# Third attention of an image tower: the order in which its token groups are combined, normalised and projected

## The reference

```python
    h = _layernorm(h + _L0_ffn_ref(h, ...), axis=-1)   # ends in the expert mixture
    h = _layernorm(h + _L1_attn_ref(h, ...), axis=-1)  # the third attention

    # _L1_attn_ref: 12 heads of 16 channels, 37 tokens an image
    qkv = jnp.einsum('bnc,oc->bno', x, w_qkv)...
    attn = jnp.einsum('bhid,bhjd->bhij', q, k) * scale[None, :, None, None]
    attn = jnp.where(diag[None, None, :, :], -jnp.inf, attn)
    attn = jax.nn.softmax(attn, axis=-1)
    out = jnp.einsum('bhij,bhjd->bhid', attn, v)
    out = out @ w_proj.T + b_proj
    return out + x
```

## Time and profile before

| | us |
|---|---|
| median of 3 runs | 1878.59 |
| the runs | 1878.59, 1874.66, 1887.67 |
| the profiled execution | 1880.07 |
| span of its instructions | 1878.3 |

### The profile page before, as it was taken

One profiled execution on the slowest core, in us unless ns is written; L12 is line 12 of the kernel. 1 busy time (PEld: TensorE's weight loads), 2 busy tenths in 40 slices (PEclk: granted clock), 3 DMA queues, 4 the chain that ended last, 5 costly groups with the idle time before them and its releaser, 6 DMA issues.

```text
span 1878.3 us, 33999 instructions
## 1 busy us (share of the span) xinstructions
PE 1609.9 (86%) x11941; PEld 1493.8 (80%) x11941; DVE 1067.8 (57%) x2975; ACT 812.7 (43%) x1979; POOL 512.2 (27%) x1259
## 2 busy tenths in 40 slices
PE   5898995984988998899977999788989999789980
PEld 5787874984877898889977999688878898779970
DVE  4665555332654777457765444367755778634437
ACT  2453531432555554345433555344543544245520
POOL 3255244004432121522232000453126123300031
PEclk8765855995557999999889999879989989899995
DMA  5020001551088000100004676300011000167731
GB/s 154 26 78 28 25 21 54 149 161 27 24 269 249 2 1 18 47 18 1 16 16 133 202 224 216 96 15 2 1 48 34 1 11 20 29 191 229 224 94 35
DMA packets 87756, 149.78 MB, mean 80 GB/s; under 512 B 7380, under 2 KB 58883, under 8 KB 87590
## 3 DMA queue, kind: packets, MB, share of 16 engines
q1 hardware_dynamic: 81254, 135.35, 23.6%
q0 software_dynamic: 6336, 12.26, 2.3%
HBM read 106.59 MB, written 41.05 MB: 79 GB/s over the span
## 4 chain that ended last, share of the span: by engine, by line
PE 54%; issue 22%; DVE 16%; ACT 4%; POOL 2%; DMA 2%; DVEq 0%; POOLq 0%; SPq 0%; ACTq 0%
PE ps_proj L1065 10%; PE ps_proj L1188 6%; PE ps_score L1259 5%; PE ps_proj L1079 5%; PE ps_proj L1242 4%; PE ps_o L1160 4%; PE ps_pt L1030 4%; PE ps_score L1116 4%; PE ps_o L1150 3%; PE ps_score L1127 2%; DVE prob L1593 2%; DVE prob L1590 2%; DVE negmax L1592 2%; PE ps_proj L1046 1%; PE ps_turn L1008 1%
## 5 line engine op out<-in xcount | busy, mean ns | idle before, releaser
L1259 PE MATMUL ps_score<-w,hid 128*112 128x192 f32 (+2 forms) x1680 | 300.2, 330 | 6.9 <-DVE x L1902 6.9
L1259 PEld LDWEIGHTS ps_score<-w,hid 128*112 128x112 f32 (+2 forms) x1680 | 272.8, 177 | 8.9 <-DVE x L1902 8.7
L1383 ACT ACTIVATE hid<-ps_proj 128x224 f32<-128x224 f32 (+2 forms) x360 | 137.8, 385 | 267.7 <-PE ps_proj L1242 267.7
L1490 POOL TENSOR_SCALAR tmp<-rs,var 111x1 f32<-111x1 f32 x110 | 40.5, 368 | 607.2 <-DVE rs L1561 606.8
L1448 POOL DMA_INDIRECT tin<-rows_out,idx x66 | 67.3, 1019 | 467.1 <-issue 363.8
L1030 PE MATMUL ps_pt<-const,prob 111*111 111x111 f32 x660 | 126.7, 310 | 36.7 <-ACT probt L1371 24.8
L1188 PE MATMUL ps_proj<-wo,ot 128*111 128x192 f32 (+1 forms) x616 | 141.5, 380 | 3.9 <-ACT ot L1349 3.7
L1030 PEld LDWEIGHTS ps_pt<-const,prob 111*111 111x111 f32 x660 | 94.8, 202 | 56.8 <-issue 23.7
L1371 ACT ACTIVATE probt<-ps_pt 111x333 f32<-111x333 f32 x176 | 78.8, 448 | 127.1 <-PE ps_pt L1030 126.6
L1160 PEld LDWEIGHTS ps_o<-v,probt 111*111 111x111 f32 x1056 | 126.1, 191 | 0.4
L1188 PEld LDWEIGHTS ps_proj<-wo,ot 128*111 128x111 f32 (+1 forms) x616 | 113.8, 206 | 15.5 <-issue 12.8
(11 more groups left out here) (256 smaller groups left out, 4212.2 us busy)
## 6 DMA issues: line engine op xcount, KB each, us to landing
w_in<-w_all_dram SPq DMA_DIRECT2D x130, 384.0 KB, 3.5
w<-w_all_dram SPq DMA_DIRECT2D x50, 576.0 KB, 5.2
rows_in<-zero SPq DMA_DIRECT2D x1, 12320.0 KB, 46.1
rows_out<-zero SPq DMA_DIRECT2D x1, 9240.0 KB, 79.9
tin<-rows_in SPq DMA_DIRECT2D x36, 224.0 KB
rows_out<-tout SPq DMA_DIRECT2D x36, 168.0 KB
patch<-patches_dram SPq DMA_DIRECT2D x11, 333.0 KB, 3.0
wo<-wo_all_dram SPq DMA_DIRECT2D x6, 576.0 KB, 3.9
```

The costliest lines, as they stand in the source:

```text
L1259: last = pe.matmul(bank[0:n, 0:C], hid[:, i % 2, m, at:at + n], w2[:, slot, m, :], start=(m == 0), stop=(m == FC - 1))
L1383: act.activation(hid[:, i % 2, m, 0:n], bank[:, 0:n], ACT.Relu if b.tile is None else ACT.Gelu).then_inc(taken, 1)
```

## The change

The blocks of the third attention become (0), (1,2), (3,4), (5,6,7), (8,9,10). Ahead of its first scores now stand: GAT 0, 1, 2, then COMB 0, COMB 1, NC 0, A 0, COMB 2, GAT 3, 4, 5, NC 1, the projections of block 0 and V 0, then A 1, NC 2, A 2. In round 0, QK of block 1 moves from the end of the round to right behind GAT 6, COMB 3, GAT 7. The table `DIAG_COMB` says which groups are combined in which round: one a round, but groups 6 and 7 both in round 3. NC c and A c come a round later, and A now always stands in `slots[1]`, ahead of PV. Nothing that is computed changes.

```diff
-DIAG_BLOCKS = [(0, 1), (1, 2), (3, 2), (5, 2), (7, 2), (9, 2)]
+DIAG_BLOCKS = [(0, 1), (1, 2), (3, 2), (5, 3), (8, 3)]
+DIAG_COMB = {0: [3], 1: [4], 2: [5], 3: [6, 7], 4: [8], 5: [9], 6: [10]}
...
         if a == DIAG:
+            for c in DIAG_COMB.get(n - 1, ()):
+                slots[0].append(("prev", ("NC", c)))
+                slots[1].append(("A", c))
             if n == 0:
-                slots[0] += combine(1) + combine(2) + [x for g in (1, 2) for x in (("prev", ("NC", g)), ("A", g))]
-            else:
-                slots[0] += [("prev", ("NC", n + 2))] * (n + 2 < G)
-            if n + 3 < G:
-                slots[0 if n else 2] += combine(n + 3)
-            if n and n + 2 < G:
-                slots[1 if last else 2].append(("A", n + 2))
+                slots[0].append(("prev", ("GAT", 6)))
+            for c in DIAG_COMB.get(n, ()):
+                slots[0] += combine(c)
         if n + 1 < G:
             slots[2].append(("V", n + 1, 0))
         if a == DIAG and last and b + 1 < len(s.blocks):
-            slots[2] += [("QK", b + 1, j) for j in (0, 2, 1, 3)]
+            slots[0 if n == 0 else 2] += [("QK", b + 1, j) for j in (0, 2, 1, 3)]
...
-    out = neigh_lead() if a == NEIGH else first_block(a) if last_stage[0] == "ffn" else []
+    out = neigh_lead() if a == NEIGH else []
+    if a == DIAG:
+        out += first_block(a) + [("A", 1), ("prev", ("NC", 2)), ("A", 2)]
...
-    out += [("GAT", 0), ("GAT", 1), ("COMB", 0), ("GAT", 2), ("GAT", 3), ("NC", 0), ("GAT", 4), ("next", ("A", 0))]
+    out += [("GAT", 0), ("GAT", 1), ("GAT", 2), ("COMB", 0), ("COMB", 1), ("NC", 0), ("next", ("A", 0)), ("COMB", 2),
+            ("GAT", 3), ("GAT", 4), ("GAT", 5), ("NC", 1)]
```

## The result

| us | before | after |
|---|---|---|
| median of 20 runs each, timed in turn | 1888.12 | 1877.63 |
| lowest to highest | 1873.97 to 1895.85 | 1863.73 to 1887.08 |
| the profiled execution | 1880.07 | 1864.46 |
| span of its instructions | 1878.3 | 1862.7 |

The ratio is 0.9949, with a 95% interval of 0.9930 to 0.9969. That is 9.6 us off 1888.12 (5.9 to 13.2), where 7.2 had been forecast; 1877.63 lies in the range of 1862 to 1880, within 1% as the 0.92 said. It lies near the upper end, though the gain was larger than forecast, because the kernel before now has a median of 1888.12 where the three runs that the forecast started from had 1878.59. The ratio is what tests the forecast: 1872 for 1878.59 is 0.9965. The profiled execution of the new kernel is nearly the fastest of its 20 runs.

The account below looks back on a forecast made before the run. Third attention: a chain through all engines before 464 us, then PE, mostly at 1.2 GHz. Terms -10.7 (head) + 6.0 (rounds 3, 4) + 1.3 (wide QK) - 3.8 (rest) = -7.2 us, forecast 1872, 8 in 10 within 1862 to 1880.

Parts of the forecast that it names:

- the 0.92: Whole kernel: the forecast chance that the measured time changes by less than 1%, 18.8 us, either way.
- The head: Third attention up to S 1: S 0 4.8 us later, S 1 10.7 us earlier, that lead kept at S 3.
- Rounds 3 and 4: PE waits on DVE at OT 2 and A 7, and on ACT for group 7's norm: +6.0 us together.
- the wide QK: End of round 4: QK of block 3, three groups wide, costs 20 x 0.06 = 1.3 us more.
- the list of signs: Expected in the new trace: S 0 near 444, S 1 near 453, waits at OT 2 (round 3) and A 7, 80 QK matmuls.
- Rounds 5 to 10: One QK block fewer -4.2 us, one turn wait fewer -1.4, a short round lost +1.8: net 3.8 us less.
- one such short round is lost: Rounds 5 to 10: the round behind a QK block is short from a higher clock; one block fewer costs 1.8 us.
- its bound of 5.6: Rounds 5 to 10: upper end of the forecast saving, bounded at 2 to 5.6 us less.
- The lead given back: Round 4: turns and POOL norms stall PE another 5 us, net gain 0 to 2, about 1878; chance 0.17.
- T5 starting at the low clock: Start of T5: clock stays at 0.5, costing some 11 us, net +4, 1883; chance 0.09.
- Stalls covered or the clock helps: Rounds 3 and 4 cost nothing, gain 13.2 us, or 15 with a full-clock stretch: about 1864; chance 0.2.

Follow-up runs that it names:

- the mended kernel: The changed kernel with COMB 6 and COMB 8 behind QK at the end of rounds 2 and 4, and A 7 behind PV 3; ratio 0.9904, rerun 0.9911.

## Why the prediction was right, and where a step was not

**The head: right.** The norm on POOL was forecast 1.3 us later. The first projection came 13.5 us behind the first gather, 12.1 before, so 1.4 later. S 0 was forecast 4.8 us later and came 5.0 later; S 1 10.7 earlier, and came 9.9 earlier (458.38 - 426.65 = 31.73, where it was 463.57 - 421.90 = 41.67). Round 1 was 1.0 us shorter (7.84 for 8.81), and the lead at S 3 was 10.9. The runs bear out the reason: the head alone has 10.6 at S 3, and QK's place is 1.0 of the gain at S 1. That the first profile agrees to 0.2 us is luck. The eleven profiles with the new head have S 3 between 52.4 and 58.4 us behind the first gather, with a median of 55.4; against the one profile of before that is a lead of 7.6 to 13.6, and of 10.6 at the median. What moves it is the late ACT in round 0 and the clock in rounds 1 and 2 (20.6 to 23.4 us), which the forecast took as fixed. In absolute time S 0 stood at 449.15 rather than "near 444" only because the first gather came 4.75 us later in that profile.

**Rounds 3 and 4, and the wide QK: right in the waits, and in sum partly by luck.** Foreseen were a wait at OT 2 of 1.8 us on DVE (1.62), a wait at A 7 of about 2 (2.02), something for ACT behind NC 7 before OT 2's bank is emptied (0.8; the wait at Y 2 is 1.30), and 1.3 for three groups' width. The three waits lie in round 4, that at OT 2 too, which the list of signs put in round 3. PE's idle time there went from 0.6 to 6.5 us, 5.9 more, which is what the 6.0 priced. The lead at S 5 had to be 10.7 - 6.0 - 1.3 = 3.4, and it is 3.5. That this agrees so well is luck again, for two more terms cancelled: round 3 took 10.0 us where it took 8.15, since it ran wholly at the low clock (0.50 for 0.68), a loss that the sum had put at the back, and round 4 had a stretch at the full clock (0.67) that paid for it. Two experiments bear out the waits: with blocks of two those at OT 2 and A 7 are not there and round 4 has nearly its old length (15.0), and in the mended kernel, where two of the three are gone, S 5 comes 7.0 us earlier than in the changed kernel of the same job. Of these 7.0, however, 4.5 are the clock in round 4.

On the wide QK: the step of 0.28 us for three groups at the low clock held again (matmuls of block 3 start at 507.06, 507.34, 507.62 and 507.90). The Trainium skill, "TensorE: Matmul & The Clock Gate", section "Wait — 56ns, not 53.3ns?", gives the columns over 1.2 GHz as the spacing at the low clock; for two groups' 224 columns that is an estimate of 187 ns. In the timeline of the changed kernel run again, matmuls of that width start at 450.84, 451.05, 451.26 and 451.48, 0.21 us apart: the row decides, as the sum took it, and merging blocks does save on PE. By these rows 60 matmuls at 0.213 become 40 at 0.28, which saves 1.6 us and not 2.0. And one group's 112 columns are no quicker than two's: in the changed kernel they start at 440.35, 440.56, 440.78 and 440.99, again 0.21 us apart. A block of one group costs PE as much as a block of two, which is what the split of the last block paid.

**Rounds 5 to 10: right in sign, the size wrong.** -3.8 us was forecast and the profile shows -10.1 (58.10 for 68.25). The step that failed is "with one block fewer, one such short round is lost, 1.8 us": I counted full-clock stretches as one to a QK block. They are not tied to blocks, and here they fell well. The waits at the turns were as forecast in sum: before, 1.43 us in round 7 and 1.98 in round 8 (the first is in the earlier trace rows); after, 1.99 in round 7 alone, 1.4 less. After the wait of round 7 the clock is high through much of rounds 8 to 10:

```profile
530.75:549.57 18.82, 15.65 (x98) 12.67 (x97) 7.34 (x21) 10.45 (x27) 4.80 (x24) 0.58 1.03 327
549.57:570.93 21.36, 20.74 (x206) 17.15 (x206) 12.80 (x37) 13.36 (x36) 4.45 (x22) 0.75 0.93 289
```

Rounds 8 to 10, with the same 206 matmuls, took 26.01 us at 0.55 in the kernel with T5's turn moved, 21.36 at 0.75 here, and 18.26 at 0.91 in the mended one. With the cold value the rest would have come to 58.1 + 26.0 - 21.4 = 62.7 us, 5.5 less than before. That is 1.7 beyond the forecast, within its bound of 5.6. So by this estimate 4.6 of the 6.3 us missed are this clock, and they vary from profile to profile of the same program (21.4 and 18.3).

**The total.** The profile's 13.6 us in the stage is therefore a favourable case, and the timed 9.6 (5.9 to 13.2) the better figure. The forecast of 7.2 is inside that interval, and so is 9.0, what the profile's stage gives with the cold rest (13.6 - 4.6). The parts, timed, came out differently from the sum, though within their intervals: the head alone 7.2 us (1.9 to 12.5) where it had 10.7, and the blocks of three nothing (4.5 either way) where it had a loss of 3.5 (6.0 + 1.3 - 3.8). The runs can't tell whether both terms were right or both too large and cancelled. That the clock's place averages out so over the runs is an inference. No run shows the clock of the unprofiled ones, and the blocks of three on their own (1.0000 timed, 9.5 us shorter stage profiled) say that it can't be read off one profile.

**The rivals.** The lead given back: not so, 3.5 us of it were left at S 5 and the timed gain is above 5.9. The split of the last block shows how a lost gain looks (0.9987), by another way than that rival's: a block more. T5 starting at the low clock: it did not, as its first 20 us show, with the clock and busy time of the earlier trace rows:

```profile
570.93:590.93 20.00, 19.40 (x136) 17.15 (x136) 7.44 (x19) 11.61 (x28) 5.86 (x22) 0.93 1.02 311
```

Stalls covered or the clock helps: the stalls weren't covered. The clock did help, in the profiled execution, whose gain of 15.6 us is about the 15 of that rival, but not to that extent in the timed runs, whose interval ends at 13.2.

## What to carry to other kernels

When the first work of a stage passes through a chain of engines, price the chain for all the groups that the first dense stretch needs, not for the first alone: here S 0 came 5.0 us later and S 1 9.9 earlier. Where two items are moved into one round to make a wider block, look at which engine that round was filled by, and put the second item behind the block's end: together with parting the two turns that was worth another 0.6% in the same job. A stretch in which PE sets the pace has its length from the clock it is granted, so a wait of 2 us taken from PE there is not a gain of 2 us until timed runs say so (in one job 0.9929 without it and 0.9911 with it, in another 0.9889 and 0.9911). And a part of a sum that agrees with one profile is not yet confirmed: look at a second profile of the same program.

## What the runs showed of the hardware

- One program, one order of instructions, and the stage took 144.3 and 141.8 us, in another program 134.7 and 131.7. Nearly all of it lies where the granted clock changes between 0.5 and 1.0, and in ACT's late start in round 0.
- In round 0 ACT began 3.17 us after what it reads was in place, and DVE shortly before that 1.6 us late. Six of eleven profiles with the new head have this on both engines, with "remote" as the releaser, and it comes and goes with the same program. Where the clock was then up in rounds 1 and 2, the time was made up by S 3 (55.5 for 55.1). The two don't hang together: with the late start and the clock low S 3 stood at 58.2 and 58.4, without it and with the clock up at 52.4 twice.
- The same 206 matmuls of rounds 8 to 10 took between 18.3 us (clock 0.91) and 26.0 us (0.55), in profiles whose programs differ in one or two places in earlier rounds, or, from 18.3 to 21.4, not at all. The low value came three times, each with a rise 12 to 13.4 us into round 7, once with the wait of PE there in place and twice without it; but with a rise at 12.4 us the clock also stayed up once (19.3 us).
- At the low clock the projections start 0.21 us apart with 112 columns, 0.21 with 224 and 0.28 with 336: the first group added to a block costs PE nothing, the second 0.07 us a matmul.
- The parts of the kernel that nobody touched vary by 10.2 us (up to the first gather) and 26.9 us (from T5 on) between profiles, which come from several chips. A change worth 10 us has to be read in its own stage, and timed in many runs.
